# Reordered queues in the two FP4 feed-forward stages: activation quantization first, divide ahead of scale, one unit less of lag

## The reference

```python
def fp4_quant_dequant(x):                       # blocks of 16 along the last dim
    scale = jnp.maximum(jnp.max(jnp.abs(xb), -1, keepdims=True) / 6.0, 1e-12)
    idx = jnp.searchsorted(_MID, jnp.abs(xb / scale))
    return (_GRID[idx] * jnp.sign(xb) * scale).reshape(shape)
def fp4_linear(x, w): return einsum('bsk,nk->bsn', quant(x), quant(w))
gate = fp4_linear(x, w_gate); y = fp4_linear(x, w_up)     # 352 hidden channels
return fp4_linear(jax.nn.silu(gate) * y, w_down)          # added to x
```

## Time and profile before

| | us |
|---|---|
| median of three runs | 1093.72 |
| the profiled execution, its own time | 1093.72 |
| its span in the trace | 1092.0 |
| TensorE busy (share of the span) | 940.5 (86%) |
| VectorE busy | 785.5 (72%) |
| ScalarE busy | 411.7 (38%) |
| GpSimd busy | 355.7 (33%) |

### The profile page before, as it was taken

One profiled execution on the slowest core, in us unless ns is written; L12 is line 12 of the kernel. 1 busy time (PEld: TensorE's weight loads), 2 busy tenths in 40 slices (PEclk: granted clock), 3 DMA queues, 4 the chain that ended last, 5 costly groups with the idle time before them and its releaser, 6 DMA issues.

```text
span 1092.0 us, 16451 instructions
## 1 busy us (share of the span) xinstructions
PE 940.5 (86%) x6039; PEld 556.6 (51%) x6039; DVE 785.5 (72%) x1845; ACT 411.7 (38%) x678; POOL 355.7 (33%) x449
## 2 busy tenths in 40 slices
PE   7889999899999897879999965989899668988576
PEld 3434444444344575644443423676576456767355
DVE  5578888767856557687666699765955895788784
ACT  2435656544333344334333363322312333321133
POOL 5462323312332444303223341112120444333242
PEclk9899999999999778689999977999999877986778
DMA  5372222120000000000000000000000000000000
GB/s 130 103 203 54 59 60 76 36 102 1 1 0 1 1 2 1 1 1 1 1 1 0 1 0 3 1 1 1 1 1 1 1 1 1 3 1 2 0 11 30
DMA packets 11534, 24.35 MB, mean 22 GB/s; under 512 B 1324, under 2 KB 7636, under 8 KB 11316
## 3 DMA queue, kind: packets, MB, share of 16 engines
q1 hardware_dynamic: 11152, 22.30, 7.0%
q10 hardware_dynamic: 294, 0.91, 0.3%
HBM read 15.69 MB, written 7.34 MB: 21 GB/s over the span
## 4 chain that ended last, share of the span: by engine, by line
PE 58%; DVE 30%; POOL 5%; issue 4%; ACT 2%; DMA 1%; DVEq 0%; SPq 0%; POOLq 0%; ACTq 0%
PE ps L1058 5%; PE ps L1065 4%; PE ps L1053 4%; PE ps L412 3%; PE ps L362 3%; PE ps L2599 2%; DVE XN L159 2%; PE ps L2104 2%; DVE a_MN L542 2%; PE ps L2101 2%; PE ps L382 2%; DVE st L85 2%; PE ps L1346 2%; PE ps L2629 2%; PE ps L938 2%
## 5 line engine op out<-in xcount | busy, mean ns | idle before, releaser
L542 DVE TENSOR_REDUCE a_MN<-ps 128x1 f32<-128x384 f32 (+3 forms) x154 | 93.3, 637 | 24.4 <-PE ps L365 22.7
L1275 POOL TENSOR_TENSOR f_Y<-f_Y,f_TT 128x512 f32<-128x512 f32 x48 | 60.9, 1269 | 136.1 <-DVE f_TT L1137 136.1
L112 POOL TENSOR_TENSOR rs<-t,mhalf 128x4 f32<-128x4 f32 x37 | 37.5, 1015 | 130.6 <-DVE t L95 129.1
L1229 ACT ACTIVATE f_HH<-ps,pack_zero 128x512 f32<-128x512 f32 x64 | 44.0, 687 | 95.3 <-PE ps L1053 95.3
L666 ACT ACTIVATE a_PT<-ps 128x1024 f32<-128x1024 f32 x56 | 57.3, 1024 | 57.6 <-PE ps L382 57.4
L190 DVE TENSOR_TENSOR X<-ps,X 128x512 f32<-128x512 f32 x32 | 22.0, 688 | 74.8 <-PE ps L2114 45.1
L1058 PE MATMUL ps<-f_XS,pack_zero 128*128 128x512 f32 x128 | 73.0, 653 | 0.0
L1137 DVE SCALAR_TENSOR_TENSOR f_TT<-ps,pack_zero,f_X 128x512 f32<-128x512 f32 x64 | 47.8, 747 | 33.7 <-PE ps L1065 33.2
L1065 PE MATMUL ps<-f_HH,pack_zero 128*128 128x512 f32 x128 | 65.8, 596 | 5.0 <-DVE f_TT L1137 5.0
L1053 PE MATMUL ps<-f_XS,pack_zero 128*128 128x512 f32 x128 | 67.7, 611 | 0.7 <-DVE f_XS L1021 0.7
L2399 PE MATMUL ps<-pack_one,XNT 128*128 128x352 f32 x128 | 51.1, 548 | 16.1 <-ACT XNT L182 8.6
(11 more groups left out here) (337 smaller groups left out, 2255.1 us busy)
## 6 DMA issues: line engine op xcount, KB each, us to landing
scratch<-a_parts SPq DMA_DIRECT2D x16, 384.0 KB, 3.7
a_QS<-scratch SPq DMA_DIRECT2D x14, 288.0 KB
a_KS<-scratch SPq DMA_DIRECT2D x42, 96.0 KB
pack_one<-in_one SPq DMA_DIRECT2D x1, 2694.5 KB, 9.7
pack_zero<-in_zero SPq DMA_DIRECT2D x3, 884.5 KB, 4.5
X<-in_x SPq DMA_DIRECT2D x4, 256.0 KB, 10.3
out_x<-X SPq DMA_DIRECT2D x4, 256.0 KB, 2.1
a_QS<-a_MT SPq DMA_DIRECT2D x42, 4.0 KB
```

Source lines behind the costliest of these rows:

```text
L542: dve.tensor_reduce(M.a_MN[:, n % 2, ti, h0:h0 + k], bank(M, M.bank["a_max", n, jj], 128 * (ti + 1) * k).rearrange("p (a c) -> p a c", a=k ...
L1275: pool.tensor_tensor(M.f_Y[:, i, :], M.f_Y[:, i, :], M.f_TT[:, u % 3, :], ALU.add).then_inc(made.sem, made.tick(n, u))
```

## The change

It changes the order of work within the two stages and computes the same. (1) VectorE does `norm_back` and `quant_front` of the last block ahead of the loop, `quant_powers` in step 0 and `quant_back` in step 1 (before: steps 1 to 4); GpSimd does its `quant_divide` first, ScalarE its `quant_steps` in step 1. (2) The transpose of that block (`turn_tensor`, `turn_scalar`) moves from step 6 to step 5. (3) `down` runs two steps behind `up` in place of three, on TensorE and on ScalarE, where it stays ahead of `exact(u-1)`. (4) GpSimd's queue is `divide(u)`, then `scale(u-1)`. (5) VectorE does `leave` ahead of `grid`, and the last `leave(3)` behind the loop.

```diff
@@ quant_ffn_tensor
-        if u == 6:
+        if u == 5:
             turn_tensor(pe, S, M, n, 3, 5, M.XM, (S["x_quant"], (n, 3)))
         if u < 8:
             up(u)
-        if u >= 3:
-            down(u - 3)
+        if 2 <= u < 10:
+            down(u - 2)
@@ quant_ffn_vector
-    for u in range(11):
+    if n == 5:
+        norm_back(dve, S, M, 6, 3, M.X, M.XN)
+    else:
+        norm_back(dve, S, M, 8, 3, M.X, M.XN)
+    quant_front(dve, S, M, n, 3)
+    for u in range(10):
         if u < 8:
             up(u)
+        if u == 0:
+            quant_powers(dve, S, M, n, 3)
         if u == 1:
-            norm_back(dve, S, M, n + 1, 3, M.X, M.XN)
-        elif u == 2:
-            quant_front(dve, S, M, n, 3)
-        elif u == 3:
-            quant_powers(dve, S, M, n, 3)
-        elif u == 4:
             quant_back(dve, S, M, n, 3)
         if u == 8:
             bits(7)
+        if u >= 4 and u % 2 == 0:
+            leave(u // 2 - 2)
         if 1 <= u <= 8:
             grid(u - 1)
-        if u >= 4 and u % 2 == 0:
-            leave(u // 2 - 2)
         if n == 5 and u in (5, 7, 9):
             norm_back(dve, S, M, 7, (u - 5) // 2, M.X, M.XN)
+    leave(3)
@@ quant_ffn_scalar
-        if u == 6:
+        if u == 5:
             turn_scalar(act, S, M, n, 3)
         if u < 8:
             up(u)
-        if u >= 3:
-            down(u - 3)
+        if u == 1:
+            quant_steps(act, S, M, n, 3)
+        if 2 <= u < 10:
+            down(u - 2)
         if 1 <= u <= 8:
             exact(u - 1)
-        if u == 3:
-            quant_steps(act, S, M, n, 3)
@@ quant_ffn_gpsimd (scale and divide are now written in the loop, with the same waits)
+    quant_divide(pool, S, M, n, 3)
     for u in range(11):
+        if u < 8:
+            ... divide(u)
         if 1 <= u <= 8:
-            scale(u - 1)
-        if u < 8:
-            divide(u)
-        if u == 2:
-            quant_divide(pool, S, M, n, 3)
+            ... scale(u - 1)
         if n == 5 and u >= 4 and u % 2 == 0:
             norm_root(pool, S, M, 7, u // 2 - 2)
```

More of the change, by code:

```diff
@@ L2533, in flat @@
         return blocks(t[:, i, :, :].rearrange("p a c -> p (a c)"))
[L2535 to L2545, removed]
+    quant_divide(pool, S, M, n, 3)
     for u in range(11):
+        i, div, hq = u % 4, S["q_div"], S["q_hq"]
+        if u < 8:
+            pool.wait_ge(S["q_rate"].sem, S["q_rate"].at(n, u))
+            pool.tensor_tensor(blocks(M.q_V[:, i, :]), flat(M.q_HH, i), wide16(M.q_R[:, i, :]), ALU.mult).then_inc(div.sem, div.tick(n, u))
         if 1 <= u <= 8:
-            scale(u - 1)
-        if u < 8:
-            divide(u)
-        if u == 2:
-            quant_divide(pool, S, M, n, 3)
+            w, i = u - 1, (u - 1) % 4
+            if w >= 4:
+                pool.wait_ge(S["q_turned"].sem, S["q_turned"].at(n, 2 * (w - 4) + 1))
+            pool.wait_ge(S["q_round"].sem, S["q_round"].at(n, w))
+            pool.tensor_tensor(flat(M.q_HQ, i), blocks(M.q_V[:, i, :]), wide16(M.q_A[:, i, :]), ALU.mult).then_inc(hq.sem, hq.tick(n, w))
         if n == 5 and u >= 4 and u % 2 == 0:
```

## The result

Four runs of the changed kernel gave 1106.85 to 1113.36 us, median 1110.38; four of the kernel before, the three above and one more, 1094.84. The ratio is 1.0153, with a 95% interval of 1.0125 to 1.0183. Forecast were 1101.1 us and a range up to 1108. The profiled execution took 1113.3 (span 1111.5 against 1092.0).

A forecast was written before the change was run, and what follows sets the result against it. It took a per-unit loop through GpSimd, VectorE and ScalarE, no engine full, to bound the stages. Late first scales, shorter periods and cold clocks gave +2.8 (n=7) and +4.6 (n=5): +7.4 on 1093.72, 1101.1 us, range 1091 to 1108.

The forecast's parts named there:

- the late first scale: Start of each stage: last block's work ahead of scale(0) delays the first scale, 4.8 us in n=7, 5.8 in n=5.
- the collision: Unit loop: GpSimd's divide and VectorE's two-input rounding hold each other off; 0.77 us in one case, at most 1.345.
- The 1.1 booked for the divide inside quant_back: Before the first scale: divide(1) runs amid quant_back's two-input instructions on VectorE and adds 1.1 us.
- The period at full clock: Unit loop with TensorE nearly full: 12.5 us for two periods, 6.25 each, against 6.19 before.
- The step that failed: First transposes of a stage: TensorE, after idling, begins at 1.2 GHz; 3.0 us taken for it.
- a short one in the tail: Tail of stage n=7: a second, short TensorE start at half clock, +0.6 us.
- the 43.8 + 3.0 of the sum: Stage n=7: seven periods at 6.25 make 43.8 us, plus 3.0 for TensorE's cold start.
- the sum of the periods: Stage n=5: seven periods of 6.1 to 9.4 us make 49.4 against 52.9 before; clock adds 3.0.
- Rival (c): TensorE's gaps grow, more than one unit per stage runs at 1.2 GHz: 1110 us; chance of over +11: 0.15.
- 6.0 to 7.0 were forecast for n = 7: Sign expected in the profile after: scales in stage n=7 stand 6.0 to 7.0 us apart.
- The sign of being wrong: TensorE in the stages: the prediction is wrong if the clock stays at 0.5 for over 15 us of a stage.

The follow-up runs named there:

- filled kernel: Changed kernel plus idle-time matmuls on TensorE ahead of each down(u-2), results overwritten; ratio 1.0010 to the kernel before, both stages 138.8 us.
- the repeat: The changed kernel measured once more, unchanged; ratio 1.0142 to the kernel before, both stages 146.0 us.
- the fastest order here: Changed kernel with down three steps behind up again on TensorE and ScalarE; ratio 0.9952 to the kernel before, both stages 132.7 us.

## Why the prediction was wrong

The direction was right, and so were the late first scale and the collision. The size was not: 7.4 us forecast, 15.5 measured in the medians, 12.0 of them seen in the stages. Of the 8.1 missing, 3.4 are half clock that comes back, 1.2 the first scale of n = 5, and 3.5 lie outside the stages.

- **Part 1, the late first scale.** n = 7: 4.8 forecast, 4.9 measured. n = 5: 5.8 forecast, 7.0 measured; there the second product of up(1) waited another 1.03 for TensorE, which was not in the sum.
- **The collision.** Forecast from one case as 0.77 beside a 1.09 instruction, with the whole divide as the upper bound. Measured 1.15 (2.04 less 0.89) beside a 1.385 divide: three times fully and once by 0.43 in the eight units of n = 7, twice fully and once by 0.87 in n = 5. The 1.1 booked for the divide inside quant_back was 1.07. The term was right.
- **The period at full clock.** 6.25 forecast for n = 7. With TensorE kept warm the five periods behind the first pair are 6.2, 7.0, 6.2, 6.6 and 6.0, 6.4 on average, with the filling matmuls in them.
- **The step that failed is "Clock: TensorE idles from about 1034 until the first transposes at 1040.3, so it begins at 1.2 GHz ... I take 3.0".** The price was taken once in each stage, with 0.6 for a short one in the tail. In the trace the drop comes back, as the alternation above shows, and it lies in the loop. The periods of n = 7 are 50.7, not the 43.8 + 3.0 of the sum: 3.9 short. The filled kernel shows the cause. With the granted clock at 1.00 its five periods behind the first pair take 32.0, and those of the changed kernel 35.4: the half clock that comes back costs 3.4 there. How much of the booked 3.0 a first start really costs depends on the lag as well: with three steps it cost no period anything.
- **In n = 5 the sum of the periods held** (52.0 measured, 49.4 + 3.0 = 52.4 forecast), in part by luck. Two periods grew, 8.9 for a forecast 6.4 and 7.9 for 6.8, and four of the others came out shorter than forecast. Against the filled kernel (6.5 and 6.8 for these two) the half clock costs 2.4 and 1.1: here too it came a second time.
- **Rival (c)** names this mechanism and had 0.15. Its 1110 us, next to the measured 1110.4, are luck in the size: it booked 8 to 12 us for further starts, which cost some 4.5 (3.4 and 1.1), and 3.5 of the measured time lie outside the stages. What the trace does show of it are scales up to 9.1 apart, where 6.0 to 7.0 were forecast for n = 7. The sign of being wrong, a clock at 0.5 for over 15 us of a stage, does not serve when the stretches are added up. A mean of 0.81 over 50.7 us is some 19 us at half clock, and the kernel before had 0.78 over 49.4, some 22 us (both estimates from the two windows above).
- The rows to see it in were there: the earlier trace rows put 2.7 us of GpSimd behind each rounding, and I had counted the transposes and copies into the new loop, but not that a wait they cause lengthens them themselves.
- The Trainium skill's page "TensorE: Matmul & The Clock Gate", section HAM oscillation, describes a matmul kernel that waits for a DMA in every turn of its loop and falls back to the lower clock in every turn. The trace agrees in part: waits of 5.79, 2.48 and 2.62 us are each followed by matmuls at half clock, but the units between them run at full clock, and what TensorE waits for is GpSimd's scale.
- **The last 3.5 us** between the stages' 12.0 and the medians' 15.5: 1.0 lies between the stages; the rest lies in parts that the change does not touch, and varies from execution to execution. The interval of the ratio (13.7 to 20.0 us) does not quite reach down to 13.0. That of the repeat (9.4 to 21.6 us) does. Whether a part of it belongs to the changed kernel stays open.

## What to carry to other kernels

When an instruction is taken out of a loop's chain, walk the loop again and ask which engine's queue the next result now stands behind. Here ScalarE's copies and TensorE's matmuls took the divide's place. One step more of lag, for which the kernel already had the buffers, was worth 13.5 us in this order, and 3 to 4 in two others: price such an edit in the order in which it will stand. If TensorE enters such a loop, price its half clock once for each wait and not once for each stage; off the loop it cost nothing here. Price also a VectorE instruction with two SBUF inputs beside GpSimd's. In the fastest order here the collision alone is worth 12.8 us. Whether keeping the two apart would pay in that order was not run.

## What the runs showed of the hardware

Two reductions of 704 columns ran beside a divide in 1.81, unhindered, where one rounding of 704 with two inputs went from 0.89 to 2.04. Where VectorE's instruction was first, GpSimd's was longer too: a divide that began 0.17 into the last block's L1688 took 1.76 for 1.385, and the L1690 behind it 1.76 for 0.69 (changed kernel):

```profile
1047.28 1.76 POOL L2542 TENSOR_TENSOR q_V<-q_HH,q_R 128x704 f32<-128x704 f32 x1 [1.83 <-DVE q_R L1654]
...
1047.83 1.76 DVE L1690 SCALAR_TENSOR_TENSOR q_v<-q_e,q_v 128x512 f32<-128x512 f32 x1
```

TensorE gave the same work in less time when it was given more to do: with 27 extra matmuls per stage, the two stages took 138.8 us for 146.2.
